# Moving the second layer's keys, values and binary weights ahead of its attention, sums on VectorE alone, and queries by plain fp32 products, in a two-layer attention and expert kernel on one core

## The chip, the cores and the metric

One Trainium2 chip, of which the program uses one core: TensorE (PE), VectorE (DVE), ScalarE (ACT), GpSimd (POOL), SyncE (SP) and 16 DMA engines. The metric is the device time of one execution in microseconds, as the median of several runs. A measurement of this kernel can tell about 0.5% from no change.

## The reference, cut to what matters

Four sequences of 1024 tokens, 256 features, fp32. Two layers, each a cross-attention over 77 context rows with 16 heads, and a feed-forward part. The first feed-forward part sends each token to 4 of 32 experts and adds a shared expert; the second is a chain of three products with weights of plus and minus one.

```python
x = x + xattn(layernorm(x), ctx, ctx, mask, W_q, b_q, W_k, b_k, W_v, b_v, W_o, b_o)   # layer 0
...
# experts: top 4 of softmax(layernorm(x) @ Wg); capacity 2048 pairs an expert
out = swiglu(xg, W1[e], W2[e], W3[e]) * w[:, None]
y = y.at[tok].add(out)
...
x = x + xattn(layernorm(x), ctx, ctx, Wq, bq, Wk, bk, Wv, bv, We, be)                 # layer 1, no mask
h = s0 * dense(k0, concatenate([h, -h])); h = relu(h) * 2
h = s1 * dense(k1, h); h = relu(h) * 2; x = x + s2 * dense(k2, h)
```

## The kernel before, in words

X, the 4096 tokens as 32 tiles of 128, stays in SBUF throughout. A macro is 4 tiles, 512 tokens, and there are 8. The stages follow one another, each a block with one program for each engine, so a stage begins when every engine has left the one before; `retire` clears the semaphores behind each attention.

`front` (twice) makes what attention needs. Of each macro, DVE takes the statistics (L173, L178), POOL the power of minus one half (L184, L186), DVE writes the normalised XN (L191), PE turns it (L199), ACT copies it to XH in fp32r (L578), DVE takes the rest XL (L446), and PE makes the queries as three fp32r products of halves (XH WH, XL WH, XH WL, L714: 12 matmuls of 512 columns a macro), which ACT writes to QT with the bias (L583). Before the loop PE makes all keys (L680) and values (L691, L692) out of the context; the values make a round trip through DRAM, `v_rows`, in rows of 68 bytes (L301, L306), and POOL places them (L397). `first` marks the front of layer 0. In that one SP issues, at its end, the load of the experts' up weights (L1686, four of 4 MB). In the front of layer 1 the experts' results, `y_rows` in DRAM, 4 rows of 256 for each token, are also added to X: SP fetches half macros into four buffers G (L289), POOL adds them in pairs (L407, two adds a half macro), DVE adds the two sums to X (L516). There too the binary weights are loaded and turned into fp16 (L508 on DVE; L640, L643, L648 on ACT, in the queue of the query copies).

`attend` (twice) loops over the 32 tiles. POOL begins with a memset of two padded buffers PR (L784) and stages each tile's queries (L789); PE, DVE and ACT do scores, softmax, the products with V1 and V2, and the projection. That of layer 0 also fills `y_rows` with zeros (16 MB, L777).

`route` does gate, top 4, slots and the shared expert, macro by macro. DVE computes slots (L1128 to L1143), POOL then scatters the macro's rows to their slots, 16 indirect DMAs (L1082). XN has ROWBUFS = 4 buffers; DVE waits for the scatters of four macros back before it writes one. PE counts (L1307), does the shared expert (L1260) and the next gate (L1278). The down weights (4 MB) are loaded at the start of it. `experts` loops over 160 tiles in a PE program written out: `up` (L1475), `turn_h`, `down` (L1489), `turn_x` (L1454). Expert numbers come into PE's registers 32 at a time (L1465). `ffn` is the chain of the binary products (L1616, L1637), macro by macro.

## Time and profile before

| what | us |
|---|---|
| median of 3 runs | 1482.09 (1476.71 to 1484.38) |
| the profiled execution, its own time | 1480.69 |
| its span, first to last instruction | 1478.9 |
| front, layer 0 | 0 to 65 |
| attend, layer 0 | 65 to 261 |
| route | 261 to 519 |
| experts | 519 to 814 |
| front, layer 1 | 814 to 943.5 |
| attend, layer 1 | 943.5 to 1122.5 |
| ffn | 1122.5 to 1479 |

The stages are read off the first and last instructions of each. What bounds one says nothing of another, so that shares of the whole span are of little use here.

### The profile page before, as it was taken

The page shows a single profiled execution, that of the slowest core. Times are in us where ns is not written, and L with a number is a line of the kernel's source. Part 1 is how long each engine was busy: PE and PEld are TensorE (multiplying, and loading weights), DVE is VectorE, ACT ScalarE, POOL GpSimd, SP SyncE. Part 2 cuts the span into 40 slices and gives each one's busy share as a digit, 9 for nine tenths or more (in the row PEclk, how much of TensorE's full clock was granted, in tenths as well). Part 3 has the DMA queues.
Part 4 walks back from the last instruction along what each step waited for, and adds up shares of the span by engine and source line. Part 5 has one row for each costly group of instructions (what it writes and reads, how often), then busy time and mean ns, then how long its engine had stood idle before and what let it go on. Part 6 is the DMA issues. An engine that isn't in the chain of part 4 may idle for free. (4 is left out here: it accounts for less than half of the span.)

```text
span 1478.9 us, 27473 instructions
## 1 busy us (share of the span) xinstructions
PE 1202.4 (81%) x8656; PEld 863.9 (58%) x8656; DVE 818.5 (55%) x2098; ACT 493.4 (33%) x982; POOL 471.9 (32%) x579
## 2 busy tenths in 40 slices
PE   7689999456675289999998345499996999999998
PEld 5567777345454167778776234377773554555554
DVE  7567776455544245656565677288885334434431
ACT  3445554122122033333332113555552212222221
POOL 4311211166566435555555764122210000000000
PEclk9899999688777589999999677699998999999999
DMA  8990000422222544444442891000000000000000
GB/s 170 303 385 5 1 1 1 136 78 89 72 86 90 182 126 147 148 136 152 149 140 63 229 262 53 11 2 1 1 1 1 0 15 15 16 15 14 14 1 29
DMA packets 99408, 123.62 MB, mean 84 GB/s; under 512 B 32800, under 2 KB 74719, under 8 KB 99299
## 3 DMA queue, kind: packets, MB, share of 16 engines
q1 hardware_dynamic: 85475, 87.82, 20.4%
q0 software_dynamic: 13824, 34.38, 6.2%
q8 instruction: 65, 1.06, 0.3%
q14 instruction: 44, 0.36, 0.1%
HBM read 61.62 MB, written 64.72 MB: 85 GB/s over the span
## 5 line engine op out<-in xcount | busy, mean ns | idle before, releaser
L1616 PE MATMUL psA<-H,B 128*128 128x512 f16 x1024 | 223.5, 379 | 0.0
L1541 DVE SCALAR_TENSOR_TENSOR H<-psA,H 128x512 f16<-128x512 f32 x128 | 88.3, 690 | 209.7 <-ACT H L1584 209.7
L1367 POOL DMA_INDIRECT y_rows<-YB,pair x160 | 155.5, 972 | 145.4 <-issue 84.9
L1475 PE MATMUL psH<-W,XT 128*128 x640 | 169.9, 389 | 9.7 <-issue 9.2
L1616 PEld LDWEIGHTS psA<-H,B 128*128 128x128 f16 x1024 | 100.3, 98 | 119.2
L1584 ACT ACTIVATE H<-psA 128x512 f16<-128x512 f32 x128 | 76.4, 597 | 253.8 <-PE psA L1616 253.8
L1082 POOL DMA_INDIRECT x_rows<-XN,slot_s x128 | 126.1, 985 | 90.8 <-DVE slot_s L1143 53.0
L866 ACT ACTIVATE PHT<-psT 128x512 f16<-128x512 f32 (+1 forms) x192 | 93.5, 521 | 117.0 <-PE psT L926 116.9
L807 DVE TENSOR_REDUCE mx<-psS 128x8 fp32r<-128x616 f32 x128 | 101.5, 795 | 50.1 <-PE psS L905 48.2
L1475 PEld LDWEIGHTS psH<-W,XT 128*128 128x128 f32 x640 | 111.9, 195 | 20.6 <-issue 11.6
L814 DVE TENSOR_TENSOR PLT<-psT,PHT 128x512 f16<-128x512 f32 (+1 forms) x192 | 109.5, 597 | 25.2 <-ACT PHT L866 25.2
L184 POOL TENSOR_SCALAR var<-mv 128x4 f32<-128x4 f32 x32 | 8.7, 272 | 325.0 <-DVE mv L178 324.9
L789 POOL COPY QS<-QT 128x256 f32 (+1 forms) x64 | 25.6, 400 | 252.7 <-PE psS L905 248.4
L1379 ACT ACTIVATE XT<-psX 128x256 f32<-128x256 f32 x160 | 61.5, 384 | 133.0 <-PE psX L1454 89.2
L199 PE MATMUL psX<-ident,XN 128*128 128x128 f32 x256 | 42.0, 318 | 78.0 <-DVE XN L191 78.0
L858 ACT ACTIVATE PR<-psS 128x616 f32<-128x616 f32 x128 | 88.5, 693 | 45.7 <-PE psS L914 42.0
L926 PE MATMUL psT<-ident,PR 128*128 128x128 f32 x640 | 98.2, 285 | 4.3 <-DVE PLT L814 3.9
L1431 DVE COPY HT<-psT 128x128 f32<-128x128 f32 x159 | 46.4, 292 | 99.8 <-PE psT L1483 79.0
L1489 PE MATMUL psY<-W,HT 128*128 x320 | 97.3, 387 | 0.0
L914 PE MATMUL psS<-mx,minus_ident 128*128 128x312 f32 x256 | 74.4, 374 | 15.8 <-DVE mx L807 15.8
L199 PEld LDWEIGHTS psX<-ident,XN 128*128 128x128 f32 x256 | 36.0, 166 | 86.3 <-DVE XN L191 58.7
L926 PEld LDWEIGHTS psT<-ident,PR 128*128 128x128 f32 x640 | 68.8, 142 | 25.3 <-issue 19.8
(227 smaller groups left out, 2327.6 us busy)
## 6 DMA issues: line engine op xcount, KB each, us to landing
XG<-x_rows SPq DMA_DIRECT2D x160, 134.0 KB
y_rows<-zero_row SPq DMA_DIRECT2D x4, 4096.0 KB, 27.2
G<-y_rows SPq DMA_DIRECT2D x16, 1024.0 KB, 8.9
x_rows<-zero_row SPq DMA_DIRECT2D x33, 134.0 KB, 7.5
X<-in_x SPq DMA_DIRECT2D x8, 512.0 KB, 4.6
W<-in_w SPq DMA_DIRECT2D x1, 4096.0 KB, 16.3
out_x<-OUT SPq DMA_DIRECT2D x8, 512.0 KB, 2.9
y_rows<-YB,pair POOLq DMA_INDIRECT x160
```

What stands on the lines that cost most here:

```text
L199: last = pe.transpose(psX[:, c, t * P:(t + 1) * P], XN[:, t, c * P:(c + 1) * P], ident[:])
L807: dve.tensor_reduce(m, half(h), X_AXIS, ALU.max).then_inc(max_ready, 1)
L814: dve.tensor_tensor(PLT[u][:, lo:hi], piece(u, g), PHT[u][:, lo:hi], ALU.subtract).then_inc(lo_out, 1)
L858: act.activation(PR[u][:, h * HH:(h + 1) * HH, 0:KEYS].rearrange("p (r j) k -> p r j k", r=2), half(h), ACT.Exp, scale=SCALE).then_inc(exp ...
L866: act.activation(PHT[u][:, lo:hi], piece(u, g), ACT.Copy).then_inc(hi_out, 1)
L926: last = pe.transpose(piece(u, g)[:, c - lo], flat[:, c * P:(c + 1) * P], ident[:])
L1082: pool.indirect_dma_start(x_rows[:, :], bass.IndirectOffsetOnAxis(ap=slot_s[b][:, t * TOPK + k:t * TOPK + k + 1], axis=0), XN[b][:, t, :], ...
L1367: pool.indirect_dma_start(y_rows[:, :], bass.IndirectOffsetOnAxis(ap=pair[u // HALF][:, u % HALF:u % HALF + 1], axis=0), YB[u][:], None, b ...
L1475: last = pe.matmul(psH[v][:], XT[v][:, c], w13[c][:, ds(e * (2 * HID), 2 * HID)], start=c == 0, stop=c == KC - 1)
L1489: pe.matmul(psY[v][:], HT[v][:], w2[:, ds(e * D, D)], start=True, stop=True).then_inc(y_done, 1)
L1541: dve.scalar_tensor_tensor(out=H[layer][1][:, o], in0=psA[k % 4][:], scalar=0.0, in1=H[layer][0][:, o], op0=ALU.max, op1=ALU.subtract).the ...
L1616: last = pe.matmul(psA[k % 4][:], W[:, c, o * P:(o + 1) * P], src[part][:, c], start=n == 0, stop=n == 2 * n_in - 1)
```

## The change

- Keys and values of layer 1 move into `route` (class `KeysValues`): ACT permutes the weights and copies keys out at the end of macro 0 and values at the end of macro 1, PE makes keys at the end of macro 0 and values at the end of macro 1, DVE places keys after macro 1, finds the largest value after 2, places values after 4 and finishes after 5. In both layers the key bias becomes a further fp32 product of one row with a row of ones instead of a bias of the copy.
- The binary weights are loaded and converted in `experts` (class `BinaryWeights`): 24 ACT pieces of 512 columns at tiles 24 to 121, 4 DVE subtractions, 12 small DVE steps, and SP's loads at tiles 8 and 84.
- The front of layer 1 becomes `combine`: no POOL pairs, DVE adds all four results to X, macro by macro, with three buffers of a whole macro. ACT writes XN in both layers, with a scale and a shift that POOL prepares.
- The queries are plain fp32 products of WQ and XT, 4 a macro instead of 12 of halves.
- The PR memset covers only the 48 padding columns. `ROWBUFS` is 3. The experts' up weights are loaded at the start of `attend` (ahead of the zeros), the down weights in `route` after `finished`, into the space of QT. PE's expert numbers come 8 at a time into two sets of registers. One more `retire` stands between `experts` and `combine`.
- QT, KB, V, B0, B1, B2 are held throughout; parts of them serve as buffers of other stages.

```diff
-ROWBUFS = 4
+ROWBUFS = 3
-GBUFS = 4
-POOL_PAIRS = (0, 2)
-DVE_ADDS = (0, 2)
-EXPERT_LOADS = 32
+GBUFS = 3
+TOP_AT = 3
+CONVERT_AT = tuple(range(24, 72, 3)) + tuple(range(100, 124, 3))
+SUBTRACT_AT = (92, 94, 96, 98)
+SECOND_LOAD = 84
+EXPERT_LOADS = 8
+LOAD_AT = 3
...
+    class KeysValues:
...
+        def keys(self, pe):
+            pe.wait_ge(self.k_ready, 1 + KC)
+            for o in range(KC):
+                for c in range(KC):
+                    pe.matmul(self.psK[o][:, 0:BATCH * KEYS], self.WK[:, c, o * P:(o + 1) * P], ctxT[:, c, :],
+                              start=c == 0, stop=False)
+                pe.matmul(self.psK[o][:, 0:BATCH * KEYS], self.turned_row[0:1, 0, o * P:(o + 1) * P],
+                          ones[0:1, 0:1].to_broadcast([1, BATCH * KEYS]), start=False, stop=True).then_inc(self.k_done, 1)
...
+    class Queries:
...
+        def power(self, pool, m):
+            if m >= 2:
+                pool.wait_ge(self.xn_ready, m - 1)
+            pool.wait_ge(self.norm.var_ready, m + 1)
+            pool.tensor_scalar(self.shift[m % 2][:], self.norm.mv[m % 2][:, :, 0], -1.0, None, ALU.mult)
+            self.norm.power(pool, m, m % 2)
...
+        def apply(self, act, m):
+            act.wait_ge(self.shift_ready, m + 1)
+            if m >= 2:
+                act.wait_ge(self.turned, m - 1)
+            for t in range(MT):
+                last = act.activation(self.XN[m % 2][:, t:t + 1, :], X[:, m * MT + t:m * MT + t + 1, :], ACT.Identity,
+                                      bias=self.shift[m % 2][:, t:t + 1], scale=self.norm.rstd[m % 2][:, t:t + 1])
+            last.then_inc(self.xn_ready, 1)
...
+        def products(self, pe, m):
...
+            pe.wait_ge(self.x_out, m + 1)
+            for o in range(KC):
+                if m:
+                    pe.wait_ge(self.q_out, (m - 1) * KC + o + 1)
+                for c in range(KC):
+                    last = pe.matmul(self.psQ[:, o], self.WQ[:, c, o * P:(o + 1) * P], self.XT[m % 2][:, c],
+                                     start=c == 0, stop=c == KC - 1)
+                last.then_inc(self.q_done, 1)
...
-                        terms = [(W, XX, c) for c in range(KC) for W, XX in ((WH, XH), (WH, XL), (WL, XH))]
-                        for n, (W, XX, c) in enumerate(terms):
-                            last = pe.matmul(psQ[:, o], W[:, c, o * P:(o + 1) * P], XX[m % 2][:, c],
-                                             start=n == 0, stop=n == len(terms) - 1)
-                        last.then_inc(q_done, 1)
...
+    def combine(w):
...
+                def fetch(m):
+                    if m >= GBUFS:
+                        sp.wait_ge(summed, m - GBUFS + 1)
+                    sp.dma_start(G[m % GBUFS][:], rows_of(m, 0, MT)).then_inc(fetched[m % GBUFS], 16)
+                for h in range(2):
+                    sp.dma_start(G[0][:, 2 * h:2 * h + 2, :], rows_of(0, 2 * h, 2 * h + 2)).then_inc(halves[h], 16)
...
+                def add_up(m, lo, hi):
+                    x = X[:, m * MT + lo:m * MT + hi, :]
+                    for k in range(TOPK):
+                        own.done(dve.tensor_tensor(x, x, G[m % GBUFS][:, lo:hi, k * D:(k + 1) * D], ALU.add))
...
+                for m in range(MACROS):
+                    if m + 1 < MACROS:
+                        q.high(act, m + 1)
+                    if m + 2 < MACROS:
+                        q.apply(act, m + 2)
+                    q.out(act, m)
...
-                    pool.memset(PR[u][:], 0.0).then_inc(padded, 1)
+                    pool.memset(PR[u][:, :, KEYS:KPAD], 0.0).then_inc(padded, 1)
...
+                kv.load(sp)
+                kv.store(sp)
+                kv.fetch(sp)
+                sp.wait_ge(kv.finished, 1)
                 load_down(sp)
...
                     add_shared(m)
+                    if m == 1:
+                        kv.place_keys(dve)
+                    if m == 2:
+                        kv.top(dve)
+                    if m == 4:
+                        kv.place_values(dve)
+                    if m == 5:
+                        kv.low(dve)
...
                     shared_out(m)
+                    if m == 0:
+                        kv.keys(pe)
+                    if m == 1:
+                        kv.values(pe)
...
+                    if j in CONVERT_AT:
+                        binary.convert(act, CONVERT_AT.index(j))
...
+                    up(j, u % 2, expert(j))
+                    if j % EXPERT_LOADS == LOAD_AT and j + EXPERT_LOADS < ETILES:
+                        load_experts(j - LOAD_AT + EXPERT_LOADS)
...
+        attend(layer0, True, True, load_up)
+        retire()
+        route(counts, plan_all, own_f, layer1, load_down)
+        experts(W13, W2, (w_loaded, 16 * (2 * KC + 1)), plan_all, own_f, BinaryWeights())
         moe.close()
...
+        retire()
+        combine(layer1)
+        attend(layer1, False, False, None)
```

## Rows read from the trace of the kernel before

**Rows 1.** Windows by stage: length, busy us and count per engine, clock, DMA share, GB/s.

```profile
261.00:519.00 258.00, 141.11 (x594) 105.63 (x594) 120.99 (x418) 44.99 (x58) 136.80 (x146) 0.74 0.30 105
519.00:814.00 295.00, 273.03 (x1440) 224.62 (x1440) 172.30 (x640) 104.93 (x320) 155.49 (x160) 0.96 0.43 133
814.00:943.50 129.50, 57.90 (x203) 43.43 (x203) 83.21 (x162) 37.31 (x43) 70.56 (x68) 0.71 0.54 156
```

**Rows 2.** Group by line: engine, operation, tiles, count, busy, mean ns, idle before.

```profile
L446 DVE TENSOR_TENSOR XL<-psX,XH 128x1024 fp32r<-128x1024 f32 x8 | 9.6, 1200 | 3.1 <-ACT XH L578 3.1
```

**Rows 3.** Tile G: the sum's duration in ns, min/median/max.

```profile
L516 DVE TENSOR_TENSOR X<-X,G x32: 671/748/1824, 827.8 to 909.7; 128x512 f32<-128x512 f32 x32
```

**Rows 4.** Timeline, front of layer 1: start, length, engine, line, count, idle before.

```profile
825.28 11.65 POOL L407 TENSOR_TENSOR G<-G 128x512 f32<-128x512 f32 x8 [8.85 <-DMA G<-y_rows]
...
875.96 1.40 DVE L173 BATCH_NORM_STATS2 st<-X 128x6 f32<-128x256 f32 x4
...
907.45 2.98 DVE L516 TENSOR_TENSOR X<-X,G 128x512 f32<-128x512 f32 x4
...
943.53 2.27 POOL L784 MEMSET PR<- 128x1280 f32 x2 [29.48 <-POOLq L277]
```

**Rows 5.** Windows within the fronts, columns as in rows 1.

```profile
34.00:36.00 2.00, 2.00 (x6) 1.52 (x6) 2.00 (x7) 0.00 (x0) 0.00 (x0) 0.50 0.91 82
866.00:872.00 6.00, 3.59 (x14) 3.17 (x15) 3.67 (x9) 1.02 (x1) 3.56 (x4) 0.51 1.06 382
```

**Rows 6.** Timeline of PE and its loads, front of layer 0.

```profile
10.28 0.34 PEld L680 LDWEIGHTS psK<-ctxT,W 128*128 128x128 f32 x1 [0.18 <-issue]
10.79 0.34 PEld L680 LDWEIGHTS psK<-ctxT,W 128*128 128x128 f32 x1 [0.18 <-issue]
...
22.53 0.47 PE L714 MATMUL psQ<-XH,WH 128*128 128x512 f32 x1
...
28.53 0.39 PE L714 MATMUL psQ<-XL,WH 128*128 128x512 f32 x1
28.76 0.39 PE L714 MATMUL psQ<-XH,WL 128*128 128x512 f32 x1
30.16 1.09 PE L199 MATMUL psX<-ident,XN 128*128 128x128 f32 x8 [1.01 <-DVE XN L191]
```

**Rows 7.** Value products by line; then the timeline at that front's end.

```profile
L691 PE MATMUL psK<-W,ctxT 128*77 128x256 f32 x16 | 4.3, 391 | 0.0
...
62.30 2.22 DVE L482 SCALAR_TENSOR_TENSOR V<-VC,v_scale,V 128x1920 f16<-128x1920 f32 x1 [5.88 <-ACT V L605]
```

**Rows 8.** Timeline of one macro of the route stage.

```profile
325.45 1.10 POOL L1082 DMA_INDIRECT x_rows<-XN,slot_s  x1 [5.02 <-DVE slot_s L1143]
...
327.10 1.19 PE L1278 MATMUL psG<-XH,wg 128*128 128x512 f32 x2 [9.06 <-DVE X L1154]
...
340.28 0.19 PE L1307 MATMUL psR<-chosen,before 128*128 128x32 bf16 x1
...
348.36 0.29 DVE L1128 TENSOR_TENSOR pos<-psR,counts 128x128 f32<-128x128 f32 x1 [3.68 <-remote]
...
352.48 1.10 POOL L1082 DMA_INDIRECT x_rows<-XN,slot_s  x1 [5.36 <-DVE slot_s L1143]
...
361.99 0.29 DVE L1100 TENSOR_REDUCE mx<-psR 128x4 f32<-128x128 f32 x1 [4.85 <-PE psR L1298]
```

**Rows 9.** Register loads of PE's queue, and the timeline around the second.

```profile
L1465 PEldq TENSOR_LOAD <-plan_all x5: 2240/2320/2322, 521.9 to 750.2; - x5
...
578.48 0.29 DVE L1435 TENSOR_TENSOR HB<-SG,psH 128x128 f32<-128x128 f32 x1
...
580.95 1.37 PE L1475 MATMUL psH<-W,XT 128*128 x4 [2.01 <-issue]
...
582.78 0.28 DVE L1435 TENSOR_TENSOR HB<-SG,psH 128x128 f32<-128x128 f32 x1
```

**Rows 10.** Group by line: one conversion of binary weights.

```profile
L643 ACT ACTIVATE B<-early,shrunk 128x2048 f16<-128x2048 uint8 x4 | 8.3, 2086 | 0.0
```

More of the change, by code:

```diff
@@ L9 @@
+import math
 from contextlib import ExitStack
@@ new lines, in _ @@
+                fetch_x(0)
+                kv.load(sp)
+                q.load(sp)
+                for m in range(1, MACROS):
+                    fetch_x(m)
+                sp.dma_start(mask_u[:], a["mask"].rearrange("(n p) k -> p n k", p=P)).then_inc(mask_in, 16)
+                sp.wait_ge(zeroed, 2)
+                sp.dma_start(v_rows[:, :, KEYS:KPAD, :].rearrange("b h k v -> (b h) (k v)"),
+                             zero_v[:]).then_inc(cleared, 16)
+                kv.store(sp)
+                sp.dma_start(x_rows[SLOTS:SLOTS + P, :], zero_row[:, 0:ROW]).then_inc(cleared, 16)
@@ L421, in _ @@
-                blanks()
-                for m in range(MACROS):
-                    pair_up(2 * m)
-                    pair_up(2 * m + 1)
-                    if m == 2:
-                        keys_out()
+                ready = Steps(pool, consts)
+                ready.done(pool.memset(ones[:], 1.0))
+                pool.affine_select(out=ident[:], in_=ones[:], compare_op=ALU.is_equal, fill=0.0, base=0,
+                                   pattern=[[-1, P]], channel_multiplier=1).then_inc(ident_ready, 1)
@@ new lines, in _ @@
+                pool.memset(zero_v[:], 0.0).then_inc(zeroed, 1)
+                pool.memset(head_of_pair[:], 1.0)
+                pool.memset(ones_b[:], 1.0)
+                pool.affine_select(out=ident_b[:], in_=ones[:], compare_op=ALU.is_equal, fill=0.0, base=0,
+                                   pattern=[[-1, P]], channel_multiplier=1)
+                ready.done(pool.affine_select(out=before[:], in_=ones[:], compare_op=ALU.is_gt, fill=0.0, base=0,
+                                              pattern=[[1, P]], channel_multiplier=-1))
@@ L645, in _ @@
-                    if m == 6:
-                        values_high()
-                        act.wait_ge(k0_diff, 1)
-                        act.activation(W0[:], W0[:], ACT.Copy, scale=twice[:, 0:1])
-                if first:
-                    values_high()
+                        q.high(act, m + 1)
+                    if m + 2 < MACROS:
+                        q.apply(act, m + 2)
+                    q.out(act, m)
+                    if m == 5:
+                        kv.high(act)
@@ L683, in _ @@
-                if first:
-                    turn_in(0)
-                pe.wait_ge(v_in, 16)
-                for b in range(BATCH):
-                    if b % 2 == 0:
-                        pe.wait_ge(k_out, b // 2 + 1)
-                    dst = psK[0:KEYS, b // 2, b % 2 * D:(b % 2 + 1) * D]
-                    for c in range(KC):
-                        pe.matmul(dst, ctxT[:, c, b * KEYS:(b + 1) * KEYS], wv[:, c, :], start=c == 0, stop=False)
-                    last = pe.matmul(dst, ones[0:1, 0:KEYS], rows[0:1, 2, :], start=False, stop=True)
-                    if b % 2:
-                        last.then_inc(v_done, 1)
@@ L695, in _ @@
-                if not first:
-                    turn_in(0)
-                pe.wait_ge(w_lo, KC)
-                top_at = 2 if first else 1
+                pe.wait_ge(ident_ready, 1)
+                pe.wait_ge(ctx_in, 16)
+                for c in range(KC):
+                    for b in range(BATCH):
+                        last = pe.transpose(q.psQ[:, c, b * P:b * P + KEYS], ctx[:, b, c * P:(c + 1) * P],
+                                            ident[0:KEYS, 0:KEYS])
+                    last.then_inc(ctx_turned, 1)
@@ L721, in attend @@
+    def attend(w, masked, clear_outputs, load_ahead):
         st = ExitStack()
@@ L1310, in body @@
                     shared_out(m)
+                    if m == 0:
+                        kv.keys(pe)
+                    if m == 1:
+                        kv.values(pe)
                 for m in range(MACROS):
@@ L1500, in body @@
                     if not below(j, 2):
-                        down(j - 2, u % 2, expert(r - 2))
+                        down(j - 2, u % 2, expert(j - 2))
                     if not from_end(j, ETILES, 2):
```

965 lines of the change are left out of this document (480 added, 485 removed).

## The prediction

> **What bounds the kernel now.** I read the windows by stage first. The route stage takes 258 us with PE at 141 and POOL at 137, the experts 295 with PE busy for 273, the front of layer 1 takes 129.5 in which no engine reaches 84 [rows 1]. That last stage is where time can be had; of the ffn behind it (1122.5 on) nothing changes. The groups and the timeline tell why that front is long. Its first G lands so late that POOL starts at 825.3 and needs 1.46 us for an add of 512 columns; DVE's adds of 512 take 0.671 us at least and up to 1.824 beside them, and DVE has eight XL rests and eight XN as well [rows 2 to 4]. The last add ends at 910.4 [rows 4], and 33 us later attention begins: in that time ACT runs conversions of 2.1 us [rows 10] between the query copies, and PE waits for it.
>
> **Combine against the old front of layer 1.** The old stage is 129.2 us, from 814.4 to 943.5. In the new one DVE does 4 adds of 1024 columns a macro, alone on its port. No row shows such an add; the nearest is the rest XL of 1024 columns, 1.20 us [rows 2], and twice the least 512 gives 1.34 [rows 3]. I take 1.24 with the step between, so 4.95, and 1.95 for the statistics (1.40 for four of them [rows 4], the rest for aggregates and gaps): 6.9 a macro. Start: the halves of macro 0 are the first DMAs (814.8 with the further retire, estimated 0.5), landed by about 820 as the fastest G does; two halves of 2.9 with the second's wait, and the statistics, end macro 0 near 827.5. Macro 1 needs 4 MB in all; at the 382 GB/s that G reached [rows 5] that is 11 us, so it waits about 1 us; later macros need 2.1 MB each 6.9 us, 5.5 us of transfer, hidden by three buffers. Sums end at 828.5 + 7 x 6.9 = 877. Behind them: power and shift 1.5, XN on ACT 1.6, turn 1 to 2, copy 1, then the queries of macros 6 and 7, because ACT's order puts `out(m)` behind `apply(m+2)`; at half clock then full 6.8 + 3.4, last copy 0.7: 16 (12 to 19). End 893, a gain of 50.5 (38 to 58). PE: the plain fp32 record follows from the key products. 308 columns start every 0.514 us [rows 6] at the half clock (2 cycles a column at 1.2 GHz), so 512 columns take 0.854 at half and 0.427 at full clock, and a product of 512 has two records. A macro is 8 records: 6.8 or 3.4, where 12 fp32r records at 0.23 [rows 6] took 2.8 and at half clock 5.1. With the turn (1.0, at half 2.0) PE needs 4.5 or 8.9 for a DVE macro of 6.9. In both fronts the clock stood at 0.50 and 0.51 where PE had waited [rows 5]. I expect it to change between levels and PE to keep step at about 7.2; if it were at half throughout, eight macros cost 71, 15 more than DVE's 56.
>
> **Front of layer 0.** It ended with DVE's last V piece at 64.5 [rows 7]. DVE and ACT lose XL and share XN; PE gets more: first products near 24.4 (22.5 before [rows 6], and keys now have 12 records instead of 8, 2 us), then 8 x (3.4 + 1.04) = 35.7 if it stays at full clock, last copy 0.9: 61.0. ACT needs 1.0 + 1.6 + 1.4 = 4.0 a macro, under PE's 4.5. V is finished at macro 5 to 6, hidden under the queries. Gain 3.8. At half clock throughout (34 to 36 us shows such a stretch, 0.50 [rows 5]) PE would need 71: a loss of 31. I take full clock, since the idle before that stretch, 1.0 and 1.8 us for XN and XL [rows 6], has its cause in DVE, which now has two fifths of the work (statistics 1.8 of the 4.4 that they made with XL and XN); bounds -6 to +10.
>
> **Attend, twice.** The memset of two PR took 2.27 us ahead of the first staging [rows 4]; 48 columns instead of 1280 leave about 0.2. Both times 2.0, in sum 4. The experts' up weights now compete with nothing but the zeros: 33.5 MB at 382 GB/s [rows 5] are 88 us, at two thirds of that 132, of a stage of 196, and its tiles came at one pace during the zeros and afterwards; cost 0. SP has nothing queued behind them in that stage.
>
> **Route.** What is added: PE 12 key records and 24 value records (6.2 at half clock, and 24 x 0.27 = 6.5, estimated from 16 of them in 4.3 us [rows 7]), DVE 8 key placings, two reductions of 1024 columns (2.4 by [rows 2]), ten placings of 204 columns (3, estimated by columns), V2 2.2 [rows 7], the small scale steps 1.5. If nothing hid it, 22 us. What hides it: a macro takes 27.03 us, and after the counts at 340.3 DVE stands until 348.4, POOL's last step of the earlier macro having ended at 347.1; POOL waits for slots 5.4 us; before the next gate DVE waits 4.85 and, in macro 2, PE 9.06 [rows 8]. Each piece is smaller than the gap that it lies in (values 6.5 in 9.1, placings 3 in 4.85, keys 3 to 6 in 1.9 plus macro 1's 8.6 us on DVE). Queues: on SP the stores and fetches stand before the 4 MB of down weights and before the tails, which are needed only at 488; on ACT the V1 copies wait for DVE's placing, and the next logit copy stands behind them, 1.7 us at most, into the same 8 us gap. ROWBUFS 3: XN of macro m+1 waits for the scatters of m-2, which POOL ended 5.4 us before (and the 0.3 to 2 of landing). While the value rows of 68 bytes came back the DMA engines were at 0.91 with 82 GB/s [rows 5], and the 4 MB now run beside scatters. I take +2, between 0 and 22, as the pieces fit and only DMA may not.
>
> **Experts.** Five register loads of 2.3 us held PE 2.0 us each [rows 9]; around the second the step from 578.5 to 582.8 is 4.3 instead of 1.63, and the next ones are slow at half clock. By the differences of DVE's starts over four tiles (6.51 undisturbed; 160 starts, of which two stand in [rows 9]) the four later loads cost 4.1, 4.7, 2.0 and 1.7, with the first 1.9: 14.4. In their place 19 loads of 8 registers, 0.56 each by proportion, behind `up`'s queue of 0.9 us: between 0 and 0.56 each, 0 to 10.6. I take 0.28, as about 0.3 of each old load was hidden: 5.3, a gain of 9 (3.8 to 14.4). Covers: 24 conversions of 512 columns (0.6 each, a quarter of 2.09 [rows 10]) on ACT, which is busy 105 of 295 [rows 1]; the following SG starts 0.15 late and PE needs its result 0.9 later. Without cover they cost 14. DVE's 12 steps cost 1.5 in a tile with 0.5 free: 1 at most, within the bounds. SP's four starts at tile 8 are 2 us against a lead of up to 8 tiles.
>
> **Sum.** -50.5 (the further retire in it) - 3.8 - 4 + 2 - 9 = -65.3. Span 1478.9 - 65.3 = 1413.6; with the 1.8 around it 1415.4. The profiled execution is 1.4 under the median of the runs; I predict 1416.
>
> **The rivals.** (A) Route hides nothing, or DMA holds it up: +20, 1436. For it: the stalls there have no releaser that I can name ("remote") [rows 8], so that a gap may move with the work. Against it: they end with POOL's burst in each of six macros. The old route ran at a DMA share of 0.30 [rows 1], which leaves room. The Trainium skill, page "DMA: Bandwidth & Descriptors", section "Issuing engines are not separate DMA queues", speaks against the change here: DMAs started by SP and by POOL end up on the same 16 engines and interleave, and by that the scatters would be held up by the value rows and the 4 MB, as in this rival. No row before shows scatters beside such loads. (B) The clock stays at half in both fronts: +31 and +15, 1462. For it: 0.50 in every stretch after a wait [rows 5]. Against: full clock at 28 us [rows 6]. One front alone would give 1431 to 1447. (C) The slower side: in route XN has three buffers, and if the scatters of a macro land later than 5.4 us after POOL's last, DVE waits before each XN and the next burst starts only behind the landing. It decides from that point on; to exceed the old time it must cost over 65 us, that is 13 in each of five macros. Against it: scatters move 1 KB rows at a share of 0.3. 1495. (D) The change doesn't do what it says, the expert stage pays the conversions in full (+14) and the loads (+5): 1435.
>
> **How the numbers follow.** My forecast, 1400 to 1428: 0.58. A and D together: 0.22. B in one front or both: 0.12. Better than forecast (combine's tail at full clock, first tiles of attend at full clock, as PE no longer stands 8 us): 0.06. C: 0.02. The range 1395 to 1440 leaves out B's worse half and C. About 0.5% is what a measurement of this kernel can tell from no change; faster 0.97, same 0.01, slower 0.02.
>
> **What would show it.** After: combine from about 814 minus 15, 79 us long, DVE adds of 1024 at 1.2 to 1.25, the wait for G only in macros 0 and 1, and PE's clock at both levels. Route with scatter bursts still 27 us apart. Experts' DVE starts 6.5 for four tiles over the conversion tiles, without the breaks at 32, 64, 96 and 128. Attention's first staging 0.3 us behind its start. Wrong would be a burst distance over 28, an add near 1.5, or PE at 0.5 through a front.

## The result, and the profile after

The changed kernel takes 1436.6 us (median of four runs, 1435.18 to 1438.93) where the kernel before takes 1479.4 (four runs, 1474.93 to 1484.38); the ratio is 0.9711 with a 95% interval of 0.9673 to 0.9749. Forecast were 1416 and a range of 1395 to 1440. The sign and the range held, the size did not: 43 us instead of 65 (37 to 48 by the interval). The profiled execution has a span of 1437.2.

The experiments below ran on other chips, and the two kernels don't take the same time on each. The two first profiles are called chip A here, though the record gives no chip for them; on B and C the kernel before takes 1426.5 and 1427.4 us, on D 1475.5 and 1475.9 in two series. Measured in the same way, the change gives 50.5 us on chip C and 49.3 on D. Comparisons below are made within one chip. A stage is measured from its first transfer to that of the next one, the ffn from its first statistics:

| stage | before, A | after, A | difference | forecast | before, C | after, C | difference |
|---|---|---|---|---|---|---|---|
| front of layer 0 | 64.8 | 71.6 | +6.8 | -3.8 | 63.4 | 71.5 | +8.1 |
| attend | 197.3 | 196.5 | -0.8 | -2 | 197.4 | 196.7 | -0.7 |
| route | 256.9 | 266.2 | +9.3 | +2 | 214.5 | 222.1 | +7.6 |
| experts | 295.4 | 295.3 | -0.1 | -9 | 287.6 | 280.7 | -6.9 |
| front of layer 1, combine | 129.2 | 75.7 | -53.5 | -50.5 | 129.8 | 75.8 | -54.0 |
| attend | 179.6 | 177.6 | -2.0 | -2 | 179.6 | 177.4 | -2.2 |
| ffn | 355.8 | 354.3 | -1.5 | 0 | 355.8 | 354.5 | -1.3 |
| span | 1478.9 | 1437.2 | -41.7 | -65.3 | 1428.1 | 1378.7 | -49.4 |

So of the 23.6 us that the forecast lacks, 10.6 lie in the front of layer 0, 8.9 among the experts and 7.3 in the route; the combine stage gave 3.0 more than expected. The route of the changed kernel was profiled four times on chips without the stalls described below, and its length differs there from 218.7 to 222.1 with the same code; the 222.1 of the table is the longest.

The stages of after that answer to [rows 1] (columns as there):

```profile
267.80:534.30 266.50, 145.55 (x633) 107.82 (x633) 131.37 (x448) 50.38 (x67) 137.99 (x148) 0.75 0.35 106
534.30:829.60 295.30, 277.98 (x1440) 222.62 (x1440) 177.60 (x655) 117.82 (x344) 155.48 (x160) 0.97 0.46 139
829.60:905.30 75.70, 40.39 (x132) 21.58 (x132) 53.43 (x100) 35.50 (x60) 31.95 (x33) 0.78 0.59 226
```

In the combine stage the groups by line answer to [rows 2] and [rows 3], and a few lines of its timeline to [rows 4]:

```profile
L693 DVE TENSOR_TENSOR X<-X,G 128x1024 f32<-128x1024 f32 x28 | 34.1, 1218 | 1.3 <-DMA G<-y_rows 0.6
L199 POOL TENSOR_TENSOR rstd<-var,minus_half 128x4 f32<-128x4 f32 x8 | 15.0, 1870 | 0.7
...
834.56 5.78 DVE L693 TENSOR_TENSOR X<-X,G 128x512 f32<-128x512 f32 x8 [13.74 <-DMA G<-y_rows]
...
858.95 5.49 PE L489 MATMUL psQ<-XT,WQ 128*128 128x512 f32 x8
865.15 3.60 PE L489 MATMUL psQ<-XT,WQ 128*128 128x512 f32 x8
...
884.82 4.97 DVE L693 TENSOR_TENSOR X<-X,G 128x1024 f32<-128x1024 f32 x4
...
904.33 0.69 ACT L464 ACTIVATE QT<-psQ,bias 128x512 f32<-128x512 f32 x1 [1.03 <-PE psQ L489]
```

An addition of 1024 columns takes 1.22 us (1.24 forecast), a macro 6.97 (6.9); the first rows land 5.0 us after the start; the last statistics end at 891.9, 62.3 us into the stage (62.6), and from there to the end, 905.3, it is 13.4 us (16). PE begins at half rate (5.49 for eight records) and has the full rate from the next macro on (3.60), although it waits some 2.4 us for XN before most of the later ones.

In the front of layer 0, the timeline of PE and of what it waited for (answers to [rows 6] and [rows 7]); the second block is the kernel before:

```profile
10.36 1.39 PE L295 MATMUL psK<-ones,turned_row 1*128 1x308 f32 x2
...
18.20 1.99 PE L311 MATMUL psK<-wv,ctxT 128*77 128x256 f32 x4
20.12 1.13 PE L312 MATMUL psK<-kv_rows,ones 1*77 1x256 f32 x2
...
31.88 4.31 PE L489 MATMUL psQ<-XT,WQ 128*128 128x512 f32 x8
...
46.76 5.23 POOL L338 TENSOR_TENSOR VC<-VR,head_of_pair 128x204 f32<-128x204 f32 x10
...
56.17 1.09 PE L212 MATMUL psX<-ident,XN 128*128 128x128 f32 x8 [2.13 <-ACT XN L451]
57.09 5.30 PE L489 MATMUL psQ<-XT,WQ 128*128 128x512 f32 x8
```

```profile
9.60 4.48 PE L680 MATMUL psK<-ctxT,W 128*128 128x308 f32 x8
...
16.88 1.09 PE L691 MATMUL psK<-W,ctxT 128*77 128x256 f32 x4
...
18.48 1.09 PE L691 MATMUL psK<-W,ctxT 128*77 128x256 f32 x4
```

PE was never idle for long here, yet a batch of values took 2.98 us (18.20 to 21.18) where the kernel before needed 1.60 (16.88 to 18.48), four records of 256 columns 1.99 instead of 1.09: PE ran at half rate from its first key product (8.04) into the first macro of queries (4.31 for eight records, 3.60 in the next), although the column of the granted clock reads 1.00 there in both kernels. The queries began at 31.9 and not at 24.4. The eight macros behind it took 38.7 us, forecast 35.7: POOL placed the values (5.23) ahead of a normalisation, PE waited 2.13 us for it and had half rate in the macro after.

### The profile page after: what moved, and what is told of

The parts are those of the page before. It is cut to its first block and busy times, and to the rows that moved or that the text cites. A ratio compares the mean times of both kernels' runs of the same rounds, so it can differ in the third digit from the quotient of the medians.

```text
span 1437.2 us, 27370 instructions
## 1 busy us (share of the span) xinstructions
PE 1208.0 (84%) x8592; PEld 839.1 (58%) x8592; DVE 782.1 (54%) x2039; ACT 524.8 (37%) x1064; POOL 431.6 (30%) x560
## 5 line engine op out<-in xcount | busy, mean ns | idle before, releaser
L197 POOL TENSOR_SCALAR var<-mv 128x4 f32<-128x4 f32 x32 | 13.2, 413 | 287.1 <-DVE mv L191 286.0
L1546 PE MATMUL psY<-QT,HT 128*128 x320 | 98.7, 390 | 0.2
L1101 POOL DMA_INDIRECT x_rows<-XN,slot_s x80 | 79.8, 997 | 61.6 <-DVE slot_s L1166 30.9
L1515 PE MATMUL psX<-ident,XG 128*128 128x128 f32 x320 | 62.2, 277 | 26.3 <-DMA XG<-x_rows 26.3
L1477 DVE TENSOR_SCALAR YB<-psY,to_gate 128x256 f32<-128x256 f32 x160 | 77.1, 482 | 9.1 <-PE psY L1546 8.6
```

The source lines that it names most:

```text
L1101: pool.indirect_dma_start(x_rows[:, :], bass.IndirectOffsetOnAxis(ap=slot_s[b][:, t * TOPK + k:t * TOPK + k + 1], axis=0), XN[b][:, t, :], ...
L1477: dve.tensor_scalar(YB[u][:], psY[u % 2][:], to_gate[u // HALF][:, u % HALF, 1:2], None, ALU.mult).then_inc(y_out, 1)
L1546: pe.matmul(psY[v][:], HT[v][:], w2[:, ds(e * D, D)], start=True, stop=True).then_inc(y_done, 1)
```

## Experiments

### The key bias on ACT

Ahead of everything else: does the half rate come from what the change put between the key products?

```
-    for c: pe.matmul(psK[o][:, 0:308], WK[...], ctxT[:, c, :], start=c == 0, stop=False)
-    pe.matmul(psK[o][:, 0:308], turned_row[0:1, ...], ones.to_broadcast([1, 308]), start=False, stop=True)
+    for c: pe.matmul(psK[o][:, 0:308], WK[...], ctxT[:, c, :], start=c == 0, stop=c == KC - 1)
...
-    act.activation(KT[:, o], psK[o], ACT.Copy)
+    act.activation(KT[:, o], psK[o], ACT.Identity, bias=k_bias[:, o:o + 1])
```

The bias is turned into a column by four one-column products ahead of the key products (0.98 us from 7.43 on), so PE also starts 0.6 us earlier.

> The changed kernel, but in the front of layer 0 the bias of the keys is added by ACT when it copies them (as the kernel before did), so that PE has four products with one column instead of two pairs of one-row products with 308 columns between the key products. In the changed kernel PE ran at half rate from its first product to 31.7 us: a batch of values took 2.98 us there, against 1.60 before, and the queries began at 31.9 instead of the 24.4 forecast. Theory: the one-row products between the key products keep PE's rate low. Then the rate rises near 14 us as in the kernel before, a batch of values takes 1.6, the queries start at 24 to 25, the front ends at 64 to 65 instead of 71.6, and the whole is 7 us shorter (1430). Rival: the rate rises late for a reason that has nothing to do with the keys; then only the 2.8 us of the one-row products go, the values still take 2.98, and the front ends near 69 (1434).

Measured on chip B: 1367.05 us, the kernel before 1426.47 beside it, ratio 0.9587 (0.9557 to 0.9617); the changed kernel, which was not timed on this chip, has 0.9642 (0.9614 to 0.9670) on chip C, where the kernel before takes 1427. The front ends at 62.4. With the pairs of one-row products in place it ends at 71.1 on this same chip (the next run, whose front is that of the changed kernel) and at 70.9 to 71.6 on the others. Its timeline of PE:

```profile
8.34 4.48 PE L308 MATMUL psK<-ctxT,WK 128*128 128x308 f32 x8
12.61 1.76 PE L212 MATMUL psX<-ident,XN 128*128 128x128 f32 x8
14.30 0.60 PE L491 MATMUL psQ<-ones,turned_row 1*128 1x1 f32 x4
14.84 1.09 PE L332 MATMUL psK<-wv,ctxT 128*77 128x256 f32 x4
15.86 0.65 PE L333 MATMUL psK<-kv_rows,ones 1*77 1x256 f32 x2
...
22.17 3.60 PE L510 MATMUL psQ<-XT,WQ 128*128 128x512 f32 x8
```

With eight key products in a row PE had the full rate by 14.8 us; the values took 1.60 a batch and the queries began at 22.2, earlier than forecast. The one-row products of the values stood in the stream as before and did not bring the rate down again. The theory holds, and its size was low: 8.7 us on this chip instead of 7. What it is about the pairs (their single row, or the breaks in the stream) no run separates; the arrangement is what was tested. The earlier start is not it: the kernel before starts its eight key products at 9.6 and has the full rate at 16.9 (above).

### Route without the value products

```
     if m == 1:
-        kv.values(pe)
+        pe.sem_inc(kv.v_done, 1); pe.sem_inc(kv.v_done, 1)
```

> The changed kernel without the 24 value products of layer 1 in the route stage (they stood behind macro 1); PE only gives the signals, everything behind them runs on stale numbers, so a part of the computation is left out. The second and third burst of scatters were 34.8 us apart, the others 26.8 to 28.0. Theory: the 6.5 us of products push the logits of macro 2 from 8.9 to 12.4 us behind the start of the burst, into the stretch in which no engine is served until POOL's burst is over. Then that distance is 27.1 to 27.4, the stage 259 instead of 266.5, the whole 1429. Rival: it is the transfers (the value rows of 68 bytes, stored at 335 and fetched at 349) that hold up the scatters or the signals; they stay, and so does the distance of 34 to 35 us (1436).

Measured on chip B: 1374.28 us, ratio 0.9628 (0.9597 to 0.9658), route 218.7 us. Neither theory could be told apart: on this chip no burst stood 27 us apart from the next. The eight bursts followed each other after 21 to 24 us, with only POOL's variance and root (1.6 us) between them. That is what the next runs are about. What it does say: with the value products on PE the same stage takes 219.3 on this chip (in the kernel with the key bias on ACT), so the 24 products have no price that can be seen: the difference is 0.6 us, and the same code differs by more from profile to profile.

### The two kernels again, on chips C and D

> The changed kernel itself, again. In the runs with the key bias on ACT and without the values, the eight bursts of scatters of the route stage stood back to back (178 us for all eight, 22.2 a macro), while in both first profiles they stood 27 us apart, and the kernel before took 1426 us beside them instead of 1479. Theory: the 5 us of stall behind each burst belong to the chip or the run, not to the kernel; on a chip that has them this one takes 1437 and its third burst comes 34.8 us after the second, on one without them it takes 1374 to 1382, with a route of 218 us, and the value products cost nothing there. Rival: something in the two experiments took the stall away; then this kernel shows 27 us again, wherever it runs.

> The kernel before itself, for its profile on the same chip as the other runs. Theory: where the stalls are missing its route stage takes 218 to 222 us instead of 257, with bursts 22 to 23 us apart, and all other stages are as in the first profile within 3 us, except the ffn, whose length goes with the granted clock.

Measured on chip C: the changed kernel 1376.94 us, ratio 0.9642 (0.9614 to 0.9670); the one profiled execution of the kernel before 1429.9. The expectation for it was off in two places: the route took 214.5 us and not 218 to 222, and the experts are 7.8 us shorter than on chip A, not within 3. The stalls go with the chip: all eight profiles from A and D have them, none of the six from B and C. The route stage and the experts of the kernel before on chip C, against [rows 1]:

```profile
260.80:475.30 214.50, 121.15 (x594) 92.29 (x594) 121.08 (x418) 44.77 (x58) 137.58 (x146) 0.81 0.37 126
475.30:762.90 287.60, 267.53 (x1440) 223.41 (x1440) 171.45 (x640) 105.89 (x320) 155.89 (x161) 0.96 0.45 136
```

POOL is as busy as on chip A (137.6 and 136.8 us), and the whole stage is 42 us shorter: what [rows 8] show as waits for something "remote" is not there. The route of the changed kernel is longer by 7.6 us in this profile (by 4.2 and 4.5 in the two runs among the experts below, made on the same chip with the same route code). Its timelines of POOL and of DVE on this chip show where from:

```profile
387.45 0.98 POOL L1101 DMA_INDIRECT x_rows<-B,slot_s  x1 [0.30 <-issue]
388.73 3.44 POOL L1101 DMA_INDIRECT x_rows<-B,slot_s  x1 [0.30 <-issue]
392.47 0.98 POOL L1101 DMA_INDIRECT x_rows<-B,slot_s  x1 [0.30 <-issue]
...
388.42 2.90 DVE L338 TENSOR_TENSOR QT<-QT,head_of_pair 128x204 f32<-128x204 f32 x10
```

The same place in the run with zero weights (chip C):

```profile
387.86 2.90 DVE L338 TENSOR_TENSOR QT<-QT,head_of_pair 128x204 f32<-128x204 f32 x10
388.18 1.18 POOL L1103 DMA_INDIRECT x_rows<-B,slot_s  x1 [0.30 <-issue]
389.66 1.95 POOL L1103 DMA_INDIRECT x_rows<-B,slot_s  x1 [0.30 <-issue]
```

While DVE makes the ten placings of values, POOL's scatter takes 3.44 us instead of 0.97, and another one 3.11 beside V2 (414.6). These two are 4.6 of the 7.6 us. How long the first one gets depends on where it falls: in the other four profiles from chips B and C it takes 1.95, while the one beside V2 takes 3.12 in all of them, and the two are then 3.1 us, most of the 4.2 and 4.5. On a chip where POOL sets the pace of the route, DVE's idle time is no cover: what DVE does there from SBUF to SBUF is paid by POOL. The Trainium skill, page "SBUF — State Buffer", section "SBUF: two separate sides", says that DVE and GpSimd hold a shared pair of ports one at a time, a DVE operation with two SBUF inputs (which these are) only against a GpSimd operation that reads SBUF, and that descriptors written by GpSimd wait while DVE runs a two-port operation. The trace agrees in part: each stretched scatter ends 0.84 to 0.85 us behind the end of the DVE work beside it (391.32 and 392.17 here), but in the run with zero weights a scatter of 1.18 us got through during the placings.

One more thing shows only on chips B and C. With three buffers of XN, DVE waits three times in the route for the landing of earlier scatters, 5.4, 6.2 and 8.8 us in this profile, where the kernel before never waits for them. That is the first half of the mechanism of rival C, DVE behind the landing. The second half, the burst behind DVE, did not come, and it cost nothing: when DVE waits, the slots of the next macro are ready, and POOL starts each burst 0.2 to 0.3 us after its step before.

The third run of the changed kernel, later, on chip D, which has the stalls:

> The changed kernel itself for the third time. In its first profile (bursts 27 us apart) the third burst of scatters came 34.8 us after the second; in the kernel with the three repairs, whose route stage computes the same, it came 27.6 after it on a chip with the same stalls. Theory: the 7.3 us are one of the irregular stalls in which signals of PE arrive late, not a price of the value products; on a chip with stalls this run has all its bursts 26.6 to 28.5 us apart, or one long distance at another macro, and a route of 256 to 266 us. Rival: the value products bring it about whenever the stalls are there; then the third burst is 34 to 35 us behind the second again. Where the stalls are missing, the route takes 219 to 222 us and the run tells nothing of this.

Measured: 1426.6 us, ratio 0.9675 (0.9653 to 0.9697), route and experts in its windows:

```profile
268.10:524.20 256.10, 144.61 (x633) 106.53 (x633) 131.35 (x448) 50.41 (x67) 139.55 (x147) 0.77 0.37 111
524.20:810.90 286.70, 270.63 (x1440) 222.60 (x1440) 176.68 (x655) 118.76 (x344) 155.88 (x160) 0.97 0.48 143
```

Its bursts stand 26.6 to 28.7 us apart, the third 27.65 behind the second. The largest, 28.73, is the burst in which one scatter takes 3.11 us beside V2. Four runs below start from the kernel before and have its code in these stages: their route takes 254.0 to 255.3 us on this chip, their experts 291.6 to 294.1. So the change costs 0.8 to 2.1 us in the route, about as forecast (+2), and gains 4.9 to 7.4 among the experts (forecast 9). This profile is the fastest of the four executions (1419.95 to 1429.89), so the median one has some 7 us more in places that no profile shows. The stall of chip A, from its timelines:

```profile
342.83 0.43 PE L1344 MATMUL psR<-ident,B 32*128 32x32 f32 x4
...
353.73 0.29 DVE L1123 TENSOR_REDUCE mx<-psR 128x4 f32<-128x128 f32 x1 [16.23 <-remote]
...
356.65 0.79 PE L1288 MATMUL psH<-XH,w 128*128 128x512 f32 x1 [11.79 <-ACT B L1268]
```

PE had turned the logits by 343.3, and DVE took them up at 353.7, 1.1 us after POOL's burst and the two small steps behind it were over. The values, which pushed this signal from 8.9 to 12.4 us behind the start of the burst, may have put it into the stall; on chip D, with the same order, that did not happen. Whether it is by chance or by chip A, these runs don't say: the run without the values ran on a chip without stalls.

### Among the experts: no conversions, and smaller ones

The first leaves the conversions out and fills the places of the weights with zeros.

```
-    if j in CONVERT_AT:  binary.convert(act, CONVERT_AT.index(j))
-    if j in SUBTRACT_AT: binary.difference(dve, SUBTRACT_AT.index(j))
...
+    for flat in (b0_flat, b1_flat, b2_flat): pool.memset(flat, 0.0)
```

> The changed kernel without the 24 conversions on ACT and the four subtractions on DVE among the experts; the places of the binary weights are filled with zeros by POOL in the first 8 us of the combine stage, where it waits, so a part of the computation is left out. Theory: it is the conversions (0.80 us each, where 0.6 was taken) that ate the gain of the shorter register loads: over their tiles four DVE starts lie 6.9 to 7.9 us apart instead of 6.51, an excess of 17 us in all, of which 3.4 at tile 118 was there before too. Then the stage is 12 to 14 us shorter than that of the changed kernel on the same chip, and the starts stand 6.51 apart right through the loads of eight registers. Rival: the register loads cost what the old ones did; then it is under 4 us shorter.

The second makes them half as long and twice as many.

```
-    PIECE = FEAT // 2
+    PIECE = FEAT // 4
```

> The changed kernel with conversions of 256 columns instead of 512, 48 instead of 24, two in every three tiles, and eight subtractions. In a tile of 1.63 us ACT has two gaps of 0.48 us (before SG and before XT). Theory: a piece of 0.80 does not fit into one and delays SG or XT, a piece of about 0.43 does; then the excess over 6.51 us falls from 14 to under 4 and the whole is 10 to 12 us shorter than the changed kernel on the same chip. Rival: any instruction put between SG and XT costs its tile about the same; then 48 of them cost as much as 24 or more, and the time is the same or up to 10 us longer.

Measured on chip C: 1375.81 us (ratio 0.9638, 0.9607 to 0.9669) and 1374.96 (0.9633, 0.9608 to 0.9657), against 1376.94 (0.9642). The expert stage is 281.3 and 281.8 us against 280.7. In both, what was named as theory fell, and so did the rival that register loads of 8 cost what the old ones did. Over tiles 20 to 72 and 88 to 124 the distances of DVE's starts exceed 6.51 for four tiles by 0.5 us in all with the conversions, by 0.7 without them and by 0.6 with the small ones. The groups by line of the changed kernel's first profile, and its register loads:

```profile
L1625 ACT ACTIVATE B<-k,shrunk 128x512 f16<-128x512 uint8 x16 | 12.9, 804 | 0.0
...
L1522 PEldq TENSOR_LOAD <-plan_all x20: 587/690/853, 533.7 to 796.2; - x20
```

A conversion takes 0.80 us, not 0.6, and costs nothing on chip C; a load of eight registers takes 0.69 and costs nothing either, since behind the last conversion (tile 124) and between the two groups the starts stand 6.51 apart through every load. What the stage does pay on chip C stands at tile 8, 4.8 us over the first 20 tiles, in the timelines of SP and PE of the changed kernel there:

```profile
499.69 2.46 SPq L1587 DMA_DIRECT2D s<-in_s  x3
502.21 0.44 SPq L1589 DMA_DIRECT2D k<-in_k  x1
...
510.61 0.56 PE L1515 MATMUL psX<-ident,XG 128*128 128x128 f32 x2 [3.11 <-DMA XG<-x_rows]
```

SP issues four loads there, the 1 MB of hidden weights among them, and the expert rows queued behind them come late. On chips A and D the first 20 tiles exceed by 1.2 and 1.1 us, in the two runs on B by 1.2 and 2.8. The old loads of 32 registers show best here too: in the kernel before on chip C the distances exceed only at tiles 0, 28, 32, 60, 92 and 124, by 11.4 us in all. Two more runs were planned for this stage and gave no time: the conversions left out with nothing put in the places of the weights, and the changed kernel with loads of 32 registers. So the price of the long loads was not tried in the new code.

The excess of chip A has another nature. Over the whole stage it was 19.1 us before and 18.7 after; on chip D 17.9 and 10.2. In the kernel before and in the runs with its code it lies, apart from the breaks of the old loads, in tiles 20 to 28, 48 to 64 and 112 to 124, where no conversion runs, as in this stretch of the run with the sums on DVE (chip D, the code of before):

```profile
613.88 0.38 PE L1454 MATMUL psX<-ident,XG 128*128 128x128 f32 x2
615.21 0.39 ACT L1379 ACTIVATE XT<-psX 128x256 f32<-128x256 f32 x1 [1.21 <-PE psX L1454]
```

ACT takes PE's result up 0.95 us after its end, where it takes 0.04 in an undisturbed tile. As in the route it is a signal of PE that comes late. By this measure (over 0.5 us between PE's end and ACT's start) 9 of 160 tiles are late in the kernel before on A, 6 to 8 in its runs on D, 22 in the changed kernel on A, 11 on D and 12 there with the repairs below, and none in any run on B and C. Why there are more of them on A with the change is open; both runs against the conversions ran on chip C, so a price of the conversions on a chip with late signals is not excluded.

### One part alone: the sums on DVE, the queries in fp32

Three runs on chip D take the combine stage apart, starting from the kernel before. First the sums:

```
-POOL_PAIRS = (0, 2); DVE_ADDS = (0, 2)
+POOL_PAIRS = ();     DVE_ADDS = (0, 1, 2, 3)
```

> The kernel before with one part of the change alone: POOL's pair sums of layer 1 are given to DVE, which makes four additions of 512 columns for every half macro; everything else of the front of layer 1 stays. Theory: alone on its port DVE adds in 0.67 us, so 5.4 a macro, with XL 1.2, XN 1.4 and the statistics 1.9 that makes 9.9 a macro, against the 10.3 of the kernel before, and the 33 us between the last sum and attention stay: the stage is 0 to 5 us shorter than 129.5. Then the 53 us of the change come from what was moved away, not from the sums on DVE. Rival: the stretched additions (up to 1.82 us beside POOL) were what made the stage long; then it is 20 us or more shorter.

Then the queries (XL and WL gone, XN still on DVE):

```
-    terms = [(W, XX, c) for c in range(KC) for W, XX in ((WH, XH), (WH, XL), (WL, XH))]
+    terms = [(W, XX, c) for c in range(KC) for W, XX in ((WH, XH),)]     # both float32
```

> The kernel before with another part of the change alone: the queries of both layers by plain fp32 products, without XL and WL (XN stays on DVE, the keys and values and the binary weights stay where they were). Theory: DVE has 1.2 us less in a macro and PE 0.65 us more (two records of 0.43 for each product against three of 0.23). In the front of layer 0 the rate of PE rises near 14 us as before, since the key bias is on ACT; the stage is 3 to 6 us shorter than 64.8. In the front of layer 1 DVE is bound by POOL's sums, so that stage is 5 to 12 us shorter. Together 8 to 18 us. Rival: the plain products bring PE to half rate or make it the bound; then the front of layer 0 is as long as the changed one's 71.5.

Both together, and both without the conversions of the binary weights (zeros in their places, seven conversions off ACT, the subtraction off DVE):

```
-    if m == 5: act.activation(W2, k2, ...)
-    if m >= 4: act.activation(W1[:, c:c + 2, :], k1[:, c:c + 2, :], ...)
-    if m == 6: act.activation(W0, W0, ACT.Copy, scale=twice[:, 0:1])
+    for W in (W0, W1, W2): pool.memset(W, 0.0)
```

> The kernel before with both of the parts that were tried alone: the sums on DVE and the queries by plain fp32 products. Alone they changed the front of layer 1 by 0 (129.5) and by -10.5 (118.7 instead of 129.2). Theory: each was held back by the other, POOL's pairs set the pace of one and DVE's XL that of the other; together DVE needs 5.4 + 1.4 + 1.9 = 8.7 us a macro against 10.3, and the stage is 105 to 110 us. Rival: the two add up, and the stage stays at 117 to 119.

> The same without the conversions of the binary weights in the front of layer 1 (seven on ACT, one subtraction on DVE); zeros are put in their places by POOL at the start of the stage, where it waits for the first rows, so a part of the computation is left out. Theory: the 33 us between the last sum and attention are made of these conversions (14 us on ACT, between the copies of the queries); the stage is 10 to 16 us shorter than with both parts, 92 to 98. What is then left to the 75.7 of the changed kernel is the keys and values, the later first rows and XN on DVE. Rival: the tail is DVE's own chain of XN and statistics, and the conversions lie beside it; then it is under 5 us.

Measured, the kernel before at 1475.5 to 1475.9 beside them:

| on chip D | median | ratio (interval) | front of layer 1 |
|---|---|---|---|
| sums on DVE | 1475.85 | 1.0003 (0.9994 to 1.0013) | 129.5 |
| fp32 queries | 1462.18 | 0.9917 (0.9895 to 0.9938) | 118.7 |
| both | 1463.32 | 0.9912 (0.9894 to 0.9930) | 119.0 |
| both, no conversions | 1452.49 | 0.9841 (0.9823 to 0.9858) | 109.8 |
| changed kernel | 1426.60 | 0.9675 (0.9653 to 0.9697) | 75.7 |

The sums on DVE are worth nothing by themselves, as expected; the queries alone gave 10.5 us in this stage (5 to 12 expected). My theory of the two together fell, and its rival held: it is 119.0, not 105 to 110. The timeline of DVE in the run with both shows why:

```profile
846.85 1.21 DVE L451 TENSOR_REDUCE v_ends<-VS 77x1 f32<-77x1024 f32 x1
848.09 0.16 DVE L452 SCALAR_TENSOR_TENSOR v_top<-v_ends 77x1 f32<-77x1 f32 x1
848.17 5.88 DVE L510 TENSOR_TENSOR X<-X,G 128x512 f32<-128x512 f32 x8
...
872.56 0.16 DVE L467 COPY v_scale<-psK 128x2 f32<-128x2 f32 x1 [2.58 <-PE psK L701]
872.87 7.65 DVE L510 TENSOR_TENSOR X<-X,G 128x512 f32<-128x512 f32 x8
```

In its queue the steps of the values stand between the sums: two reductions, two waits for PE (2.15 and 2.58 us), the subtraction of the weights (2.28). The last sum ends at 901.0, 92.6 us into the stage, and 26.4 us more go by until attention, with conversions of 2.1 us between the copies of the queries on ACT. Without them it is 9.2 us less, where 10 to 16 were expected. The 34 us between 109.8 and 75.7 belong to what only the whole change does, and were not taken apart further: keys and values gone, XN on ACT (8 x 1.35 us off DVE), additions of 1024 columns (4.97 a macro instead of 5.88), and the first rows fetched at the start of the stage and not 4.1 us into it.

In the front of layer 0 the fp32 queries alone, with the key bias on ACT as before, end at 62.6 instead of 63.7: 1.1 us shorter, where I had expected 3 to 6.

### Three repairs

```
+    kv with the key bias on ACT (front of layer 0)
-    if m == 5: kv.place_values(pool)        # front of layer 0; V1 by ACT
+    if m == 5: kv.place_values(dve)
+    if m == 6: kv.high_dve(dve)
...
-    if j == AHEAD: binary.load_first(sp)
+    if AHEAD <= j < AHEAD + FC: binary.load_first(sp, j - AHEAD)     # signs already in route
```

> The changed kernel with three repairs. The key bias of layer 0 on ACT (9.1 us by the experiment before). In the same front the placing of the values and V1 on DVE, which stood idle there for 47 of 71 us, instead of POOL (5.2 us ahead of a normalisation that PE waited 2.1 us for) and ACT. Among the experts the three signs are loaded in the route stage and the 1 MB of the hidden binary weights in eight pieces at eight tiles, since at tile 8 three tiny loads and the 1 MB held the expert rows up and cost 5 us. Theory: 9.1 + 3 + 4.5, so 1359 to 1362 where the changed kernel takes 1377, and the front of layer 0 ends at 58 to 60 us. Rival: the placing on DVE comes late and the waits move to the end of the front; then only the 9 and the 4.5 remain, 1363 to 1365.

Measured on chip D: 1403.58 us, ratio 0.9512 (0.9474 to 0.9551), where the changed kernel has 1426.60 and 0.9675: 23 us by the medians, 17.2 by the two profiles (15 to 18 expected, on a chip without stalls). The front of layer 0 ends at 55.8 instead of 71.5, where 58 to 60 were expected; its last lines:

```profile
39.35 2.90 DVE L359 TENSOR_TENSOR VC<-VR,head_of_pair 128x204 f32<-128x204 f32 x10
...
42.47 1.25 DVE L410 TENSOR_SCALAR V<-VC,v_scale 128x1920 f16<-128x1920 f32 x1
...
47.81 7.03 PE L517 MATMUL psQ<-XT,WQ 128*128 128x512 f32 x16
...
54.88 0.69 ACT L492 ACTIVATE QT<-psQ,bias 128x512 f32<-128x512 f32 x1 [1.03 <-PE psQ L517]
```

PE needs 33.5 us for the eight macros (21.3 to 54.8), 4.2 each. The change at tile 8 brought 0.8 us on this chip, which has little to repair there (excess of tiles 0 to 20: 0.3 against 1.1). The 4.5 us that it was meant to bring on a chip like C were not tried. This version beats both kernels.

## Why the prediction was right, and where its size was off

- **Combine: right, step by step.** Start of the sums, their length and their pace came as forecast, PE's clock showed both levels, though it changed once and not back and forth; 53.5 us instead of 50.5, most of it in the tail (13.4 us for 16), where PE had its full rate for both of the last macros and not for one. The forecast gave no share to the single parts, and the runs show that it could not have been had by adding them.
- **Front of layer 0: the step that failed** is "I take full clock", and before it "first products near 24.4". The records that the bias adds to the key products were counted (2 us); that PE would stay at half rate with them in the stream, for some 18 us longer than before, was not. 7.5 of the 10.6 us are this. The rest is POOL: "V is finished at macro 5 to 6, hidden under the queries" named the work that hides it and left out who waits behind it on POOL's queue: a normalisation (2.1 us on PE, then a macro at half rate, 1.7 more). The rival of half rate in a front had 0.12; it was half right, in the stretch ahead of the queries that it had not been priced for.
- **Attend:** 0.8 and 2.0 us instead of 2.0 each. The first staging comes 2.1 us earlier in both, 0.16 us behind the stage's start instead of 2.21 in layer 0. There the lead has shrunk to 0.8 at the 17th tile (84.2 against 85.0). What is new beside these tiles are the loads of the expert weights, which had been put at nothing; no run separates them.
- **Route:** +2 held on chip D (+0.8 to +2.1). On chip A it was +9.3, 7.8 of it in one burst, on chip C +4.2 to +7.6. The forecast counted every piece against a gap of the engine that executes it; where POOL is the bound, DVE's placings are paid in POOL's scatters. That "a gap may move with the work", the point of rival A, is what chip A may show, in that one burst; its DMA half, that the 4 MB and the value rows hold up the scatters, shows at most in the last two bursts of chip C (21.4 us apart instead of 20.9, and 20.9 and 21.2 in the two runs with the same code). Half of the mechanism of rival C was there on chips B and C, at no cost.
- **Experts:** the terms were -14.4 for the old loads, +5.3 for the new ones, conversions nothing. On chip C the old ones are worth 11.4 at most, the new loads cost 0, the conversions 0, and the four loads at tile 8, which I had put at 2 us against a lead of eight tiles, 4.8; in sum -6.9. On D it is -4.9 to -7.4. On chip A nothing is gained (-0.1) and more signals come late than before. I had taken the breaks of the kernel before for register loads where a part of them, 2.6 of the 4.7 us at tiles 60 to 68 above all, is missing on chip C.
- **Chances:** faster by over 0.5% had 0.97. The 1436.6 lies outside my own forecast of 1400 to 1428. The range held because it reached to rivals A and D; neither came as its mechanism, so that was luck. It was luck with the chip as well: the range is in us, and on chip C the same kernel takes 1377. The gain was 43 to 50 us on three chips, where 65 were forecast.

## What to carry to other kernels

Ask of each step put into an idle gap what it shares with the engine that bounds the stage, not only whether the gap is long enough; and of each step moved within a queue, who waits for what stands behind it. Before a difference of some ten us within a stage is given a cause, look whether the same code has it on another chip: here two stages changed by 8 to 42 us with the chip alone, and one by 3 us on one chip with the same code. And of a change with several parts, try the parts alone and together: here one of them was worth nothing by itself.

## What was not expected of the hardware

- PE stayed at half rate from 8.0 to beyond 31.7 us, with hardly a break in its work, when pairs of one-row products of 308 columns stood between its key products, and had the full rate by 14.8 us when eight key products stood in a row from 8.3 on. The column of the granted clock reads 1.00 in both cases; the lengths of the records (1.99 against 1.09 us for four of 256 columns) show it.
- On chips B and C a scatter of POOL that falls beside DVE's V2 takes 3.11 or 3.12 us instead of 0.97, and ends 0.84 us after it.
- Beside DVE's additions of 1024 columns, POOL's small steps take up to five times as long: the step on four columns 1.19 instead of 0.23 us, the root 1.99 instead of 1.04. Here nothing waited for them.
- On chips A and D signals of PE reach ACT and DVE late, by 1 us among the experts and by up to 10 us in the second half of a burst of scatters, until POOL is through; on B and C never. The route of the kernel before takes 257 and 254 us there and 214 on C. What holds them up was not found, and no run tried to bring it about or to avoid it.
